# Mixture-of-experts FFN on one core: one generated order for the second stage, and a last chunk summed on VectorE

## The chip, the core and the metric

The kernel runs on one core of a Trainium2 chip. The metric is the device time of one execution in microseconds (us). The kernel before was executed three times: 1330.82 us in the median, 1330.12 to 1331.53. TensorE is PE in the profile, VectorE is DVE, ScalarE is ACT, GpSimd is POOL and SyncE is SP. SP and POOL issue the DMAs.

## What is computed

```
q = relu(cond @ W3 + b3)                      # 128 batches x 512
h = relu(((64 * x + sum_tokens(x)) * q) @ W2 + b2)   # 8192 tokens x 512
shared = (silu(h @ sw_gate) * (h @ sw_up)) @ sw_down # 704 wide
routed: each token goes to its 6 best of 64 experts, at most 64 tokens an expert,
        y[e] = (silu(buf[e] @ w_gate[e]) * (buf[e] @ w_up[e])) @ w_down[e]   # 352 wide, f32
out = x + shared + sum over a token's experts of score * y
```

## The kernel before

The 8192 tokens are 16 chunks of 512. **The first stage** computes h and the routing of all chunks, and the shared expert of the eight odd chunks, whose result is added to x on VectorE and stored by SP (`load_xr`, L357, `take_down`, L837, `store_out`, L362). The x of the even chunks is copied to the output by DMA (`keep_x`), and their h goes to memory and back (`store_hT`, `load_hT`, L340).

**The second stage**, from about 672 us on, is what the change touches. It computes the shared expert of the eight even chunks (v = 8 to 15 in the code) together with the 64 experts, which go in 32 pairs p. For a chunk, TensorE does 11 tiles `gu_tile` (12 matmuls of 512 columns each, L1163 to L1165) and 4 tiles `down_tile` (17 such matmuls, L1163 to L1165 and L1270, L1271). Between two such tiles stands either a visit `experts(p)`, that is `expert_down(p - 1)` (12 matmuls, L1410) and `expert_gate_up(p)` (32 matmuls, L1387), or a `turn(p)`, that is three transposes of the product of pair p (L1396) and four of the gathered rows of pair p + 1 (L1369). There are 33 visits (the first has no down part, the last no gate part) and 32 turns.

The order is written out by hand, once for each engine, in `unit(u)` for seven chunks and `last_unit()` for the last one. A unit holds four visits, after gu tiles 2, 6 and 10 and after down tile 2. The last unit ends with visit 31 after gu tile 9, a turn after gu tile 10, down tile 0, the last visit `experts(32)`, and down tiles 1 to 3.

The shared tiles use three PSUM banks in turn, so down tile 3 waits until VectorE has taken down tile 0 (`down_taken`). VectorE takes a down tile with `take_down` (L845, a copy to the `outst` buffers in the second stage), and scales an expert pair's result by its scores with `scale_y` (L1088). Three row buffers `hg` and three result buffers `ysc` go round.

**The sums into the output** are all made by DMAs that GpSimd issues, each behind the landing of the one before (semaphore `added`), since they can meet in a row. For a pair: `gather` of the rows for pair p + 3 (L498), then `scatter`, two indirect accumulating DMAs of 64 rows each (L509, the first with `idx_pair`, the second with `idx_hi`). For a chunk: `add_out`, two accumulating DMAs of 256 rows each (L519), both issued behind the same sum, after the scatter of the third pair of the unit; in the last unit after the last scatter. `sums_after(p)` counts the sums. At the end both SP and GpSimd wait for the last sum.

SP loads the weights: `load_down(p)` (one set of buffers) behind the down matmuls of pair p - 1, `load_gate(p + 2)` and `load_up(p + 2)` (two sets) behind the gate and up matmuls of pair p, and the next chunk's h (L340) behind every fourth pair.

Of the kernel before, what the change touches and what calls it, by code (L numbers as in the profile page):

```python
# [12 lines left out]
P = 128  # L13
# [7 lines left out]
def adaln_moe_ffn_kernel(nc, x, cond, W3, b3, W2, b2, gate_w, w_gate, w_up, w_down,  # L21
# [28 lines left out]
    PPC = NP // ND  # L50
    assert P == 2 * CAP and N == CAP and TAIL == P // 2 and B == P and E == 64 and NP == PPC * ND and PPC == 4

# [10 lines left out]
    with ctx:  # L63
# [189 lines left out]
        out_stored = [sem(f"out_stored{n}") for n in range(2)]  # L253
        gathered = [sem(f"gathered{n}") for n in range(3)]
# [49 lines left out]
        def sums_after(p):  # L304


            return 2 * (p + 1) + 2 * min((p + 1) // PPC, ND - 1)

# [10 lines left out]
        def _(sp):  # L319
# [144 lines left out]
            for p in range(NP):  # L464
                if p > 0:
                    load_down(p)
                if p + 2 < NP:
                    load_gate(p + 2)
                    load_up(p + 2)
                if p % PPC == 1 and p // PPC + 1 < ND:  # L470
                    load_hT(p // PPC + 1)
            for q in range(2):
                sp.wait_ge(out_stored[q], 32 * ND)
            sp.wait_ge(s.x_kept, 16 * ND)
            sp.wait_ge(s.pads_stored, 32)
            sp.wait_ge(s.added, 16 * (2 * NP + 2 * ND))

        @block.gpsimd
        def _(pool):
# [22 lines left out]
            def after_sums(count):  # L502
                wait(pool, s.added, 16 * count)

            def scatter(p):
                for e, idx in ((0, idx_pair[0:CAP, p:p + 1]), (1, idx_hi[:, p:p + 1])):
                    pool.wait_ge(s.y_ready, p + 1)
                    after_sums(sums_after(p) - 2 + e)
# [25 lines left out]
            for p in range(NP):  # L534
                pool.wait_ge(s.y_ready, p + 1)
                if p + 3 < NP:
                    gather(p + 3)
                scatter(p)
                if (p % PPC == PPC - 2 and p < NP - 2) or p == NP - 1:
                    for half in range(2):  # L540
                        add_out(ND + p // PPC, half)
            pool.wait_ge(s.added, 16 * (2 * NP + 2 * ND))

        @block.scalar
        def _(act):
# [164 lines left out]
            def unit(u):  # L710
                v, p = ND + u, PPC * u
                silu(v, 0)
                split_a(v, 0)
                if u == 0:
                    take_rowsT(0)
                silu(v, 1)
                silu_expert(p)
                split_a(v, 1)
                silu(v, 2)
                take_rowsT(p + 1)  # L720
                split_a(v, 2)
                silu(v, 3)
                silu_expert(p + 1)
                split_a(v, 3)
                silu(v, 4)
                take_rowsT(p + 2)
                split_a(v, 4)
                silu(v, 5)
                split_a(v, 5)
                silu_expert(p + 2)  # L730
                take_rowsT(p + 3)
                split_h(u + 1)
                silu_expert(p + 3)
                take_rowsT(p + 4)

            def last_unit():
                v, p = 2 * ND - 1, NP - PPC
                silu(v, 0)
                split_a(v, 0)
                silu_expert(p)  # L740
                silu(v, 1)
                take_rowsT(p + 1)
                split_a(v, 1)
                silu(v, 2)
                silu_expert(p + 1)
                split_a(v, 2)
                take_rowsT(p + 2)
                silu(v, 3)
                silu_expert(p + 2)
                split_a(v, 3)  # L750
                take_rowsT(p + 3)
                silu(v, 4)
                split_a(v, 4)
                silu_expert(p + 3)
                silu(v, 5)
                split_a(v, 5)

            split_h(0)
            for u in range(ND - 1):
                unit(u)  # L760
            last_unit()

        @block.vector
        def _(dve):
# [68 lines left out]
            def take_down(v, j):  # L833
                dve.wait_ge(s.down_filled, J * v + j + 1)
                if v < ND:
                    dve.wait_ge(xr_loaded[j % 2], 16 * (2 * v + j // 2 + 1))
                    nc.vector.tensor_tensor(outst[:, j % 2, :], bank[(GT + j) % 3][:, :], outst[:, j % 2, :],  # L837
                                            ALU.add).then_inc(s.down_taken, 1)
                else:
                    u = v - ND  # L840
                    if u > 0:
                        dve.wait_ge(s.added, 16 * (sums_after(PPC * (u - 1) + PPC - 2) + 2))
# [236 lines left out]
            def scale_y(p):  # L1079
# [3 lines left out]
                if p >= 3:  # L1083
                    dve.wait_ge(s.added, 16 * sums_after(p - 3))
# [7 lines left out]
            def unit(u):  # L1092
                v, p = ND + u, PPC * u
                product(v, 0)
                split_a(v, 0)
                scale_y(p - 1)
                product_expert(p)
                product(v, 1)
                split_a(v, 1)
                take_eactT(p)  # L1100
                product(v, 2)
                split_a(v, 2)
                scale_y(p)
                product_expert(p + 1)
                product(v, 3)
                split_a(v, 3)
                take_eactT(p + 1)
                product(v, 4)
                product(v, 5)
                split_a(v, 4)  # L1110
                split_a(v, 5)
                scale_y(p + 1)
                product_expert(p + 2)
                take_down(v, 0)
                take_eactT(p + 2)
                for k in range(KC):
                    split_h(NCH + u + 1, k)
                take_down(v, 1)
                take_down(v, 2)
                scale_y(p + 2)  # L1120
                product_expert(p + 3)
                take_down(v, 3)
                take_eactT(p + 3)

            def last_unit():
                v, p = 2 * ND - 1, NP - PPC
                product(v, 0)
                split_a(v, 0)
                scale_y(p - 1)
                product_expert(p)  # L1130
                take_eactT(p)
                product(v, 1)
                split_a(v, 1)
                scale_y(p)
                product_expert(p + 1)
                product(v, 2)
                take_eactT(p + 1)
                split_a(v, 2)
                scale_y(p + 1)
                product_expert(p + 2)  # L1140
                product(v, 3)
                take_eactT(p + 2)
                split_a(v, 3)
                product(v, 4)
                split_a(v, 4)
                scale_y(p + 2)
                product_expert(p + 3)
                product(v, 5)
                split_a(v, 5)
                take_eactT(p + 3)  # L1150
                take_down(v, 0)
                scale_y(p + 3)
                for j in range(1, J):
                    take_down(v, j)

            for u in range(ND - 1):
                unit(u)
            last_unit()

        @block.tensor  # L1160
        def _(pe):
# [260 lines left out]
            def unit(u):  # L1422
                v, p = ND + u, PPC * u
                gu_tile(v, 0)
                gu_tile(v, 1)
                if u == 0:
                    rowsT(0)
                gu_tile(v, 2)
                experts(p)
                gu_tile(v, 3)  # L1430
                gu_tile(v, 4)
                turn(p)
                gu_tile(v, 5)
                gu_tile(v, 6)
                experts(p + 1)
                gu_tile(v, 7)
                gu_tile(v, 8)
                turn(p + 1)
                gu_tile(v, 9)
                gu_tile(v, 10)  # L1440
                experts(p + 2)
                down_tile(v, 0)
                turn(p + 2)
                down_tile(v, 1)
                down_tile(v, 2)
# [68 lines left out]
```

## Time and profile before

| what | value |
|---|---|
| median of 3 executions | 1330.82 us |
| the profiled execution | 1330.82 us, span 1329.0 us |
| PE busy | 1291.3 us, 97% |
| DVE, ACT, POOL busy | 662.7, 370.6, 172.6 us |
| granted TensorE clock, mean | 0.988 |
| chain that ended last | 95% PE |
| HBM read and written | 196.09 MB, 61.10 MB |

The span runs from the first to the last instruction of the profiled execution; 1.8 us of its time lie outside. Busy times say how long an engine worked, not whether it was waited for. The starts of the matmuls are measured, their ends are modelled (a matmul of 512 columns is listed with 0.39 us while the next one starts 0.23 us after it), so stalls of PE are read from the distance of starts.

### The profile page before, as it was taken

To read this page: it belongs to the slowest core of one execution; us is meant where nothing else is said; L and a number is where in the kernel's file an instruction comes from. 1 tells how busy PE (TensorE), PEld (TensorE's weight loads), DVE (VectorE), ACT (ScalarE), POOL (GpSimd) and SP (SyncE) were. 2 spreads that over 40 slices of the span, in tenths; PEclk is the share of its full clock that TensorE was granted. 3 is DMA by queue.
4 is the path that set the end of the run, shared out by engine and by line. 5 is a ranking of instruction groups with operands and counts; after the bars stand their busy time and mean duration, and the time that the engine had idled before them with its cause. 6 is when DMAs were issued, how large, how long until landed. Compare 5 with 4: busy or idle time off the path is not lost.

```text
span 1329.0 us, 16619 instructions
## 1 busy us (share of the span) xinstructions
PE 1291.3 (97%) x6424; PEld 962.7 (72%) x6424; DVE 662.7 (50%) x1430; ACT 370.6 (28%) x611; POOL 172.6 (13%) x131
## 2 busy tenths in 40 slices
PE   4899999999999999999999999999999999999995
PEld 3688888888888888888876666666666666666663
DVE  6685775858768585774743223232322323323221
ACT  2634343343433434443311111121211211111110
POOL 2400000000000000000001222222222122221221
PEclk7999999999999999999999999999999999999997
DMA  6424305052250423404746797997988788797973
GB/s 202 169 101 157 105 36 193 33 175 88 77 186 4 170 88 123 139 17 153 275 169 227 250 305 256 268 318 197 317 289 248 263 260 314 234 312 251 298 210 44
DMA packets 96398, 249.89 MB, mean 188 GB/s; under 512 B 17536, under 2 KB 17664, under 8 KB 94144
## 3 DMA queue, kind: packets, MB, share of 16 engines
q1 hardware_dynamic: 84288, 222.61, 46.9%
q0 software_dynamic: 12032, 26.22, 10.1%
q8 instruction: 52, 0.85, 0.3%
q14 instruction: 26, 0.21, 0.0%
HBM read 196.09 MB, written 61.10 MB: 194 GB/s over the span
## 4 chain that ended last, share of the span: by engine, by line
PE 95%; DMA 1%; DVE 1%; issue 1%; ACT 1%; SPq 0%; POOL 0%; POOLq 0%; ACTq 0%
PE bank L1163 22%; PE bank L1165 22%; PE bank L1164 22%; PE bank L1387 11%; PE bank L1410 7%; PE bank L1197 2%; PE bank L1173 2%; PE bank L1369 1%; PE bank L1271 1%; PE bank L1270 1%; PE bank L1221 1%; PE bank L1210 1%; PE bank L1211 1%; PE bank L1396 1%; DMA stage<-in_L_cond_W_dram 1%
## 5 line engine op out<-in xcount | busy, mean ns | idle before, releaser
L1163 PE MATMUL bank<-hh,gu 128*128 128x512 f32 x704 | 280.9, 399 | 0.0
L1165 PE MATMUL bank<-hh,gu 128*128 128x512 f32 x704 | 274.7, 390 | 0.0
L1164 PE MATMUL bank<-hl,gu 128*128 128x512 f32 x704 | 274.3, 390 | 0.0
L1163 PEld LDWEIGHTS bank<-hh,gu 128*128 128x128 f32 x704 | 132.6, 188 | 35.1 <-issue 9.8
L1165 PEld LDWEIGHTS bank<-hh,gu 128*128 128x128 f32 x704 | 132.2, 188 | 28.5
L823 DVE TENSOR_TENSOR prod<-bank,prod 128x512 f32<-128x512 f32 x96 | 66.2, 690 | 172.6 <-PE bank L1165 144.9
L1164 PEld LDWEIGHTS bank<-hl,gu 128*128 128x128 f32 x704 | 132.4, 188 | 25.4
L547 ACT ACTIVATE ah<-prod 128x512 fp32r<-128x512 f32 x96 | 60.7, 632 | 275.1 <-DVE prod L823 275.1
L498 POOL DMA_INDIRECT hg<-table,idx_pair x32 | 32.9, 1029 | 787.4 <-DVE idx_hi L1033 606.4
L1163 PE MATMUL bank<-sdh,ah 128*128 128x512 f32 x320 | 128.7, 402 | 0.0
L1165 PE MATMUL bank<-sdh,al 128*128 128x512 f32 x320 | 124.9, 390 | 0.0
L1164 PE MATMUL bank<-sdl,ah 128*128 128x512 f32 x320 | 124.8, 390 | 0.0
L1163 PE MATMUL bank<-xmh,w2h 128*128 128x512 f32 x256 | 105.5, 412 | 1.8 <-DVE xml L766 1.3
L1165 PE MATMUL bank<-xmh,w2l 128*128 128x512 f32 x256 | 101.3, 396 | 0.0
L1164 PE MATMUL bank<-xml,w2h 128*128 128x512 f32 x256 | 100.7, 394 | 0.0
L590 ACT ACTIVATE prod<-bank 128x512 f32<-128x512 f32 x96 | 57.3, 596 | 130.4 <-PE bank L1165 130.1
L766 DVE TENSOR_TENSOR hl<-h,hh 128x512 fp32r<-128x512 f32 x96 | 66.8, 717 | 46.4 <-ACT hh L547 46.2
L1410 PE MATMUL bank<-wd,eactT 128*64 128x512 f32 (+1 forms) x384 | 89.6, 601 | 0.0
L1088 DVE TENSOR_SCALAR ysc<-bank,hg 64x512 f32<-64x512 f32 x64 | 48.0, 750 | 69.4 <-PE bank L1410 62.0
L563 ACT ACTIVATE h<-bank,b2c 128x512 f32<-128x512 f32 x64 | 43.9, 686 | 137.2 <-PE bank L1165 137.2
L1387 PE MATMUL bank<-wg,hgt 128*64 128x352 f32 x512 | 81.3, 459 | 0.0
L1387 PE MATMUL bank<-wu,hgt 128*64 128x352 f32 x512 | 81.2, 459 | 0.0
(123 smaller groups left out, 1708.4 us busy)
## 6 DMA issues: line engine op xcount, KB each, us to landing
wg<-in_L_ffn_w_gate_dram SPq DMA_DIRECT2D x64, 704.0 KB, 9.3
wu<-in_L_ffn_w_up_dram SPq DMA_DIRECT2D x64, 704.0 KB, 10.9
wd<-in_L_ffn_w_down_dram SPq DMA_DIRECT2D x64, 512.0 KB, 5.2
x<-in_x_dram SPq DMA_DIRECT2D x16, 1024.0 KB, 8.7
table<-hrow SPq DMA_DIRECT2D x16, 1024.0 KB, 4.4
wd<-in_L_ffn_w_down_dram SPq DMA_DIRECT2D x64, 192.0 KB, 6.1
hT<-h SPq DMA_DIRECT2D x8, 1024.0 KB, 3.9
outst<-in_x_dram SPq DMA_DIRECT2D x32, 256.0 KB, 5.1
```

The costliest lines, as they stand in the source:

```text
L498: nc.gpsimd.indirect_dma_start(out=hg[p % 3][:, :], out_offset=None, in_=table, in_offset=bass.IndirectOffsetOnAxis(ap=idx_pair[:, p:p + 1 ...
L547: return nc.scalar.activation(o, i, ACT.Copy)
L563: nc.scalar.activation(h32[:, oc, :], bank[5 + oc % 2][:, :], ACT.Relu, bias=b2c[:, oc:oc + 1]).then_inc(s.cond_taken, 1)
L590: nc.scalar.activation(prod[0:m, i % 2, :], bank[t % 3][0:m, :], ACT.Silu).then_inc(s.silu_ready, 1)
L766: return nc.vector.tensor_tensor(o, full, high.bitcast(F32), ALU.subtract)
L823: nc.vector.tensor_tensor(prod[0:m, i % 2, :], bank[t % 3][up0:up0 + m, :], prod[0:m, i % 2, :], ALU.mult).then_inc(s.prod_ready, 1)
L1088: op = nc.vector.tensor_scalar(ysc[p % 3][rows, :], bank[6][rows, :], hg[p % 3][rows, at:at + 1], None, ALU.mult)
L1163: nc.tensor.matmul(o, st_h, mv_h, start=first_mm, stop=False)
L1164: nc.tensor.matmul(o, st_h, mv_l, start=False, stop=False)
L1165: return nc.tensor.matmul(o, st_l, mv_h, start=False, stop=last_mm)
L1387: op = nc.tensor.matmul(o[half, 0:I], hgt[:, k, half], w[p % 2][e][:, k * I:(k + 1) * I], start=(k == 0), stop=(k == KC - 1))
L1410: op = nc.tensor.matmul(bank[6][half, :], eactT[0:m, it, half], wd[e][0:m, it, :], start=(it == 0), stop=(it == IT - 1))
```

## The change

One generator, `second_stage()`, gives the order of the second stage to all engines. It goes through the tiles of the eight chunks and counts work done: 12/17 for a gu tile, 1 for a down tile. Visit p comes after the first tile at which the count has reached 2.0 + 2.7 p, turn p after the first at which it has reached 2.0 + 2.7 (p + 0.5) (a visit goes first where both are due). VectorE and ScalarE follow the same order. SP loads the next chunk's h after gu tile 1 of a chunk. GpSimd issues the first half of a chunk's `add_out` after down tile 1 and the second half after down tile 3, each behind the sum before it. The last chunk has no `add_out`: when the 78 sums have landed, SP loads its four slices of 128 rows from the output into the `outst` buffers, VectorE adds each down tile to its slice in `take_down`, and SP stores the slice. ScalarE's list is generated in the same way and is left out here, as are the removed hand-written lists.

```diff
--- before.py
+++ after.py
@@ -48,6 +48,7 @@
+    GU_SHARE, FIRST_EXPERTS, EXPERTS_APART = 12 / 17, 2.0, 2.7
@@ -301,10 +303,34 @@
-        def sums_after(p):
-            return 2 * (p + 1) + 2 * min((p + 1) // PPC, ND - 1)
+        def second_stage():
+            done, p, turned = 0.0, 0, 0
+            for v in range(ND, 2 * ND):
+                for n in range(GT + J):
+                    yield ("gate_up", v, n) if n < GT else ("down", v, n - GT)
+                    done += GU_SHARE if n < GT else 1.0
+                    if v == ND and n == 1:
+                        yield "rows", 0, 0
+                    if p <= NP and done >= FIRST_EXPERTS + p * EXPERTS_APART:
+                        yield "experts", p, 0
+                        p += 1
+                    elif turned < p and turned < NP and done >= FIRST_EXPERTS + (turned + 0.5) * EXPERTS_APART:
+                        yield "turn", turned, 0
+                        turned += 1
+        sums, after_scatter, after_add = 0, {}, {}
+        for kind, n, j in second_stage():
+            if kind == "experts" and n > 0:
+                sums += 2
+                after_scatter[n - 1] = sums
+            if kind == "down" and n < 2 * ND - 1 and j % 2 == 1:
+                sums += 1
+                after_add[n, j // 2] = sums
+        SUMS = sums
@@ -461,19 +487,28 @@  (sync)
-            for p in range(NP):
-                if p > 0:
-                    load_down(p)
-                if p + 2 < NP:
-                    load_gate(p + 2)
-                    load_up(p + 2)
-                if p % PPC == 1 and p // PPC + 1 < ND:
-                    load_hT(p // PPC + 1)
+            for kind, n, j in second_stage():
+                if kind == "gate_up" and j == 1 and n + 1 < 2 * ND:
+                    load_hT(n + 1 - ND)
+                if kind == "experts" and 0 < n < NP:
+                    load_down(n)
+                if kind == "experts" and n + 2 < NP:
+                    load_gate(n + 2)
+                    load_up(n + 2)
+
+            sp.wait_ge(s.added, 16 * SUMS)
+            at = chunk_of(2 * ND - 1) * CH
+            for j in range(J):
+                rows = of[at + j * P:at + (j + 1) * P, :]
+                sp.dma_start(down_place(2 * ND - 1, j), rows).then_inc(last_loaded[j], 16)
+            for j in range(J):
+                rows = of[at + j * P:at + (j + 1) * P, :]
+                sp.wait_ge(s.down_taken, J * (2 * ND - 1) + j + 1)
+                sp.dma_start(rows, down_place(2 * ND - 1, j)).then_inc(out_stored[j % 2], 16)
@@ -499,22 +534,18 @@  (gpsimd)
             def add_out(v, half):
                 pool.wait_ge(s.down_taken, J * v + 2 * half + 2)
-                after_sums(sums_after(PPC * (v - ND) + PPC - 2 if v < 2 * ND - 1 else NP - 1))
+                pool.wait_ge(s.added, 16 * (after_add[v, half] - 1))
@@ -531,15 +562,15 @@
-            for p in range(NP):
-                pool.wait_ge(s.y_ready, p + 1)
-                if p + 3 < NP:
-                    gather(p + 3)
-                scatter(p)
-                if (p % PPC == PPC - 2 and p < NP - 2) or p == NP - 1:
-                    for half in range(2):
-                        add_out(ND + p // PPC, half)
-            pool.wait_ge(s.added, 16 * (2 * NP + 2 * ND))
+            for kind, n, j in second_stage():
+                if kind == "experts" and n > 0:
+                    pool.wait_ge(s.y_ready, n)
+                    if n + 2 < NP:
+                        gather(n + 2)
+                    scatter(n - 1)
+                if kind == "down" and (n, j // 2) in after_add and j % 2 == 1:
+                    add_out(n, j // 2)
+            pool.wait_ge(s.added, 16 * SUMS)
@@ -832,14 +826,16 @@  (vector)
-                if v < ND:
-                    dve.wait_ge(xr_loaded[j % 2], 16 * (2 * v + j // 2 + 1))
-                    nc.vector.tensor_tensor(outst[:, j % 2, :], bank[(GT + j) % 3][:, :], outst[:, j % 2, :],
+                if v < ND or v == 2 * ND - 1:
+                    if v < ND:
+                        dve.wait_ge(xr_loaded[j % 2], 16 * (2 * v + j // 2 + 1))
+                    else:
+                        dve.wait_ge(last_loaded[j], 16)
+                    nc.vector.tensor_tensor(down_place(v, j), bank[(GT + j) % 3][:, :], down_place(v, j),
                                             ALU.add).then_inc(s.down_taken, 1)
@@ -1089,73 +1085,21 @@
-            def unit(u):
...
-            for u in range(ND - 1):
-                unit(u)
-            last_unit()
+            for kind, n, j in second_stage():
+                if kind == "gate_up" and (j % 2 == 1 or j == GT - 1):
+                    product(n, j // 2)
+                    split_a(n, j // 2)
+                    if j == GT - 1 and n + 1 < 2 * ND:
+                        for k in range(KC):
+                            split_h(NCH + n + 1 - ND, k)
+                if kind == "experts":
+                    scale_y(n - 1)
+                    if n < NP:
+                        product_expert(n)
+                if kind == "turn":
+                    take_eactT(n)
+                if kind == "down":
+                    take_down(n, j)
@@ -1483,9 +1373,17 @@  (tensor)
-            for u in range(ND - 1):
-                unit(u)
-            last_unit()
+            for kind, n, j in second_stage():
+                if kind == "gate_up":
+                    gu_tile(n, j)
+                if kind == "down":
+                    down_tile(n, j)
+                if kind == "rows":
+                    rowsT(0)
+                if kind == "experts":
+                    experts(n)
+                if kind == "turn":
+                    turn(n)
```

## Rows read from the trace of the kernel before

**Rows 1.** Busy time by stretch: from:to, length, busy of each engine, clock, DMA share, GB/s

```profile
1100.00:1200.00 100.00, 100.00 (x511) 65.75 (x509) 29.41 (x50) 17.46 (x32) 23.68 (x18) 1.00 0.87 285
1200.00:1300.00 100.00, 100.00 (x521) 62.86 (x519) 30.88 (x53) 15.51 (x28) 23.64 (x18) 1.00 0.76 241
1300.00:1329.00 29.00, 12.91 (x57) 9.65 (x53) 3.57 (x5) 0.00 (x0) 5.35 (x4) 0.76 0.31 46
```

**Rows 2.** Timeline of PE, a visit, gu tiles and a turn: start us, duration us, instruction

```profile
1019.96 2.80 PE L1410 MATMUL bank<-wd,eactT 128*64 128x512 f32 x12
...
1027.42 0.50 PE L1163 MATMUL bank<-hh,gu 128*128 128x512 f32 x1
...
1028.00 0.39 PE L1165 MATMUL bank<-hh,gu 128*128 128x512 f32 x1
...
1032.77 0.40 PE L1165 MATMUL bank<-hh,gu 128*128 128x512 f32 x1
1033.00 0.49 PE L1396 MATMUL bank<-ident,eact 128*128 128x128 f32 x3
...
1033.73 0.48 PE L1163 MATMUL bank<-hh,gu 128*128 128x512 f32 x1
```

**Rows 3.** Timeline of the end, all engines

```profile
1298.33 2.80 PE L1410 MATMUL bank<-wd,eactT 128*64 128x512 f32 x12
...
1301.17 1.51 DVE L1088 TENSOR_SCALAR ysc<-bank,hg 64x512 f32<-64x512 f32 x2 [2.05 <-PE bank L1410]
...
1303.44 1.40 POOL L509 DMA_INDIRECT out_dram<-ysc,idx_pair  x1 [6.50 <-DVE ysc L1088]
...
1309.13 1.40 POOL L509 DMA_INDIRECT out_dram<-ysc,idx_hi  x1 [4.29 <-DMA out_dram<-ysc,idx_pair]
...
1312.52 0.39 PE L1271 MATMUL bank<-sdl,ah 128*128 128x512 f32 x1
1312.95 0.69 DVE L845 COPY outst<-bank 128x512 f32<-128x512 f32 x1 [3.16 <-PE bank L1271]
1313.33 2.56 POOL L519 DMA_DIRECT2D out_dram<-outst  x2 [2.80 <-DMA out_dram<-ysc,idx_hi]
```

**Rows 4.** The chain that ended last, in order of time: start us, us, what

```profile
1303.44 4.94 DMA out_dram<-ysc,idx_pair
...
1309.13 3.67 DMA out_dram<-ysc,idx_hi
```

**Rows 5.** DMA to landing of the output's DMAs from 1290 us on

```profile
DMA to landing us min/median/max: 3.7/5.4/8.3
```

**Rows 6.** The program's last line, L63: ns min/median/max, first and last start us

```profile
L63 POOLq COMPARE_BRANCH  x1: 41/41/41, 1322.4 to 1322.4; - x1
...
L63 POOLq DRAIN  x1: 6193/6193/6193, 1322.6 to 1322.6; - x1
L63 SPq DRAIN  x1: 13/13/13, 1322.7 to 1322.7; - x1
L63 SPq EVENT_SEMAPHORE  x1: 17/17/17, 1329.0 to 1329.0; - x1
```

**Rows 7.** Loads of x slices, 256 KB each (line L357)

```profile
DMA to landing us min/median/max: 2.6/5.1/8.8
```

**Rows 8.** Stores of output slices, 256 KB each (line L362)

```profile
DMA to landing us min/median/max: 2.0/4.2/8.6
```

**Rows 9.** VectorE on a down tile (tile outst): ns min/median/max

```profile
L837 DVE TENSOR_TENSOR outst<-bank,outst x32: 672/691/692, 119.1 to 680.1; 128x512 f32<-128x512 f32 x32
```

**Rows 10.** Timeline of POOL over one pair and one chunk's add_out

```profile
985.15 1.01 POOL L498 DMA_INDIRECT hg<-table,idx_pair  x1 [7.88 <-DVE ysc L1088]
986.46 1.42 POOL L509 DMA_INDIRECT out_dram<-ysc,idx_pair  x1 [0.30 <-issue]
996.04 1.40 POOL L509 DMA_INDIRECT out_dram<-ysc,idx_hi  x1 [8.16 <-DMA out_dram<-ysc,idx_pair]
1000.20 2.56 POOL L519 DMA_DIRECT2D out_dram<-outst  x2 [2.76 <-DMA out_dram<-ysc,idx_hi]
...
1011.59 1.50 POOL L509 DMA_INDIRECT out_dram<-ysc,idx_pair  x1 [4.79 <-DMA out_dram<-outst]
```

**Rows 11.** DMA issues, 1000 to 1200 us: count, KB each, median us to landing

```profile
wd<-in_L_ffn_w_down_dram SPq DMA_DIRECT2D x20, 192.0 KB, 6.3
out_dram<-outst POOLq DMA_DIRECT2D x6, 512.0 KB, 8.0
...
hg<-table,idx_pair POOLq DMA_INDIRECT x10, 8.0
```

More of the change, by code:

```diff
@@ L253, in adaln_moe_ffn_kernel @@
         out_stored = [sem(f"out_stored{n}") for n in range(2)]
+        last_loaded = [sem(f"last_loaded{n}") for n in range(J)]
         gathered = [sem(f"gathered{n}") for n in range(3)]
@@ L302, in logits_bank @@
             return bank[3] if n % 2 == 0 else bank[6]
-        def sums_after(p):
-            return 2 * (p + 1) + 2 * min((p + 1) // PPC, ND - 1)
+        def second_stage():
[12 more added lines that the diff above has]
+                        turned += 1
+            assert p == NP + 1 and turned == NP
+        sums, after_scatter, after_add = 0, {}, {}
[7 more added lines that the diff above has]
+        SUMS = sums
         def down_place(v, j):
@@ L462, in _ @@
             store_out(v, 3)
-            for p in range(NP):
-                if p > 0:
-                    load_down(p)
-                if p + 2 < NP:
-                    load_gate(p + 2)
-                    load_up(p + 2)
-                if p % PPC == 1 and p // PPC + 1 < ND:
-                    load_hT(p // PPC + 1)
+            for kind, n, j in second_stage():
[15 more added lines that the diff above has]
+                sp.dma_start(rows, down_place(2 * ND - 1, j)).then_inc(out_stored[j % 2], 16)
             for q in range(2):
-                sp.wait_ge(out_stored[q], 32 * ND)
+                sp.wait_ge(out_stored[q], 32 * (ND + 1))
             sp.wait_ge(s.x_kept, 16 * ND)
             sp.wait_ge(s.pads_stored, 32)
-            sp.wait_ge(s.added, 16 * (2 * NP + 2 * ND))
         @block.gpsimd
@@ L500, in gather @@
                     in_offset=bass.IndirectOffsetOnAxis(ap=idx_pair[:, p:p + 1], axis=0)).then_inc(gathered[p % 3], 16)
-            def after_sums(count):
-                wait(pool, s.added, 16 * count)
             def scatter(p):
+                pool.wait_ge(s.y_ready, p + 1)
                 for e, idx in ((0, idx_pair[0:CAP, p:p + 1]), (1, idx_hi[:, p:p + 1])):
-                    pool.wait_ge(s.y_ready, p + 1)
-                    after_sums(sums_after(p) - 2 + e)
+                    wait(pool, s.added, 16 * (after_scatter[p] - 2 + e))
                     nc.gpsimd.indirect_dma_start(
@@ L533, in _ @@
             pool.wait_ge(s.x_kept, 16 * ND)
-            for p in range(NP):
-                pool.wait_ge(s.y_ready, p + 1)
-                if p + 3 < NP:
-                    gather(p + 3)
-                scatter(p)
-                if (p % PPC == PPC - 2 and p < NP - 2) or p == NP - 1:
-                    for half in range(2):
-                        add_out(ND + p // PPC, half)
-            pool.wait_ge(s.added, 16 * (2 * NP + 2 * ND))
+            for kind, n, j in second_stage():
[7 more added lines that the diff above has]
+            pool.wait_ge(s.added, 16 * SUMS)
         @block.scalar
@@ L708, in silu_expert @@
                 nc.scalar.activation(esilu[:, :], bank[3][:, 0:I], ACT.Silu).then_inc(s.esilu_ready, 1)
-            def unit(u):
[L711 to L714, printed above, removed]
-                    take_rowsT(0)
[L716 to L758, printed above, removed]
-            for u in range(ND - 1):
-                unit(u)
-            last_unit()
+            split_h(0)
+            for kind, n, j in second_stage():
+                if kind == "gate_up":
+                    if j % 2 == 0:
+                        silu(n, j // 2)
+                    if j % 2 == 1 or j == GT - 1:
+                        split_a(n, j // 2)
+                    if j == GT - 1 and n + 1 < 2 * ND:
+                        split_h(n + 1 - ND)
+                if kind == "rows":
+                    take_rowsT(0)
+                if kind == "experts" and n < NP:
+                    silu_expert(n)
+                if kind == "turn":
+                    take_rowsT(n + 1)
         @block.vector
@@ L834, in take_down @@
                 dve.wait_ge(s.down_filled, J * v + j + 1)
-                if v < ND:
-                    dve.wait_ge(xr_loaded[j % 2], 16 * (2 * v + j // 2 + 1))
-                    nc.vector.tensor_tensor(outst[:, j % 2, :], bank[(GT + j) % 3][:, :], outst[:, j % 2, :],
+                if v < ND or v == 2 * ND - 1:
[4 more added lines that the diff above has]
+                    nc.vector.tensor_tensor(down_place(v, j), bank[(GT + j) % 3][:, :], down_place(v, j),
                                             ALU.add).then_inc(s.down_taken, 1)
                 else:
-                    u = v - ND
-                    if u > 0:
-                        dve.wait_ge(s.added, 16 * (sums_after(PPC * (u - 1) + PPC - 2) + 2))
+                    if v > ND:
+                        dve.wait_ge(s.added, 16 * after_add[v - 1, j // 2])
                     elif j < 2:
@@ L1083, in scale_y @@
                 if p >= 3:
-                    dve.wait_ge(s.added, 16 * sums_after(p - 3))
+                    dve.wait_ge(s.added, 16 * after_scatter[p - 3])
                 for e in range(2):
@@ L1090, in scale_y @@
                 op.then_inc(s.y_ready, 1)
[L1092 to L1154, printed above, removed]
@@ L1156, in _ @@
-            for u in range(ND - 1):
-                unit(u)
-            last_unit()
+            for kind, n, j in second_stage():
+                if kind == "gate_up" and (j % 2 == 1 or j == GT - 1):
+                    product(n, j // 2)
+                    split_a(n, j // 2)
+                    if j == GT - 1 and n + 1 < 2 * ND:
+                        for k in range(KC):
[8 more added lines that the diff above has]
+                    take_down(n, j)
@@ L1420, in turn @@
                 rowsT(p + 1)
[L1422 to L1445, printed above, removed]
-                experts(p + 3)
-                down_tile(v, 3)
-                turn(p + 3)
-            def last_unit():
-                v, p = 2 * ND - 1, NP - PPC
-                gu_tile(v, 0)
-                gu_tile(v, 1)
-                experts(p)
-                gu_tile(v, 2)
-                turn(p)
-                gu_tile(v, 3)
-                gu_tile(v, 4)
-                experts(p + 1)
-                gu_tile(v, 5)
-                turn(p + 1)
-                gu_tile(v, 6)
-                experts(p + 2)
-                gu_tile(v, 7)
-                turn(p + 2)
-                gu_tile(v, 8)
-                gu_tile(v, 9)
-                experts(p + 3)
-                gu_tile(v, 10)
-                turn(p + 3)
-                down_tile(v, 0)
-                experts(NP)
-                for j in range(1, J):
-                    down_tile(v, j)
             v = ND - 1
@@ L1485, in _ @@
             pe.wait_ge(s.slots_ready, 1)
-            for u in range(ND - 1):
-                unit(u)
-            last_unit()
+            for kind, n, j in second_stage():
+                if kind == "gate_up":
+                    gu_tile(n, j)
+                if kind == "down":
+                    down_tile(n, j)
+                if kind == "rows":
+                    rowsT(0)
+                if kind == "experts":
+                    experts(n)
+                if kind == "turn":
+                    turn(n)
 _INS = ['x', 'cond_1024', 'L0_cond_W3', 'L0_cond_b3', 'L0_cond_W2', 'L0_cond_b2', 'L0_ffn_gate_w',
```

## The prediction

> **What bounds the kernel now.** I read the busy time by stretch first. In the second stage PE is busy 100.00 of every 100 us at a granted clock of 1.00, the full one of its two levels, 2.4 GHz [rows 1]. Since ends of matmuls are modelled, I then looked in the timeline at their starts: the 21 steps from 1028.00 to 1032.77 us take 4.77 us, so 0.227 us for each shared matmul, and the next item follows without a gap [rows 2]. Prices of the stage: a gu tile 12 x 0.227 = 2.7 us, a down tile 17 x 0.227 = 3.9 us, a visit 1027.42 - 1019.96 = 7.5 us, a turn 33.73 - 33.00 = 0.7 us [rows 2]. No DMA, bank or engine is waited for, although the DMA engines are busy 0.87 of the time. So no new order can make this stage shorter; it can only keep it or put stalls into it. What can be gained stands behind the matmuls: of the last 29.0 us PE works 12.91 [rows 1]. The timeline shows this end as a chain: the last visit's down part is over at 1298.33 + 2.80 = 1301.1, scale_y runs from 1301.17, the last pair's first scatter is issued at 1303.44 and the second at 1309.13, and only then, at 1313.33, the two halves of the last chunk's sum, although PE's last matmul started at 1312.52 and VectorE took its tile from 1312.95 [rows 3]. The second half is issued some 0.8 us after the first and takes the longest landing of this stretch, 8.3 us [rows 5], which puts it at 1322.4: there GpSimd's last wait ends, and a drain of GpSimd of 6.19 us follows before the closing barrier at 1329.0 [rows 6].
>
> **The change, part by part.**
>
> *The order on PE.* The same items in another order: 88 gu tiles, 32 down tiles, 33 visits, 32 turns, all still between shared tiles. Visits come 2.7 units of work apart, where a unit of work is 3.9 us (a down tile), so with 8.2 us for visit and turn about every 10.4 + 8.2 = 18.6 us, against 11.76 / 4 = 2.94 units or 19.6 us in the units before. I take 0 us for PE: its work is the cover and ends at 1312.5 + 0.4 = 1312.9 as before. The waits that could break this are costed next.
>
> *Weights.* The cover of their loads shrinks. Placing the tiles by the generator's rule, the shortest distance between two visits is 16.0 us (a visit, two down tiles and a turn, as between visits 20 and 21). The down weights are the tight ones: issued when the down matmuls are through, 2.8 us into a visit, landing 6.3 us after issue in the median [rows 11]; with about 2 us to issue the four they are there some 11 us into the distance. The cover is about 5 us; cost 0. Demand rises by 19.6 / 18.6, so the DMA share of 0.87 to about 0.91. The h of the next chunk is asked for after gu tile 1 and needed after gu tile 10: over 30 us.
>
> *VectorE and ScalarE.* Each follows PE's order, so neither waits for something that PE does later. The new place that matters is behind gu tile 10, where four splits of h now stand ahead of the take of down tile 0. The splits cost about 4 x 0.7 = 2.8 us and down tile 3 needs that take only three down tiles or 11.6 us after gu tile 10; cost 0.
>
> *GpSimd's sums.* This is a chain of landings, off PE's path but near its pace. A pair takes 1.3 us for the gather, 996.04 - 986.46 = 9.6 us for the first scatter and 4.2 us for the second; both halves of an add_out, issued together, 1011.59 - 1000.20 = 11.4 us [rows 10]. A pair is 15.1 us, or 13.8 where the queue lags, since the gather is then issued under a landing. Before: 4 x 15.1 + 11.4 = 72 us of a unit's 4 x 19.6 = 78. After: the halves stand singly, up to 8.0 us each [rows 11], and there are 11.76 / 2.7 = 4.36 pairs in a chunk: 4.36 x 13.8 + 16 = 76.2 us, at the lagging price, of 78 + 0.36 x 8.2 = 81 us. This fits, with 5 us to spare. When the queue lags, gathers are late first: a gather takes 8.0 us to land [rows 11] and is needed a distance and a half later, which leaves 12 us or more. Cost 0, with the other end of this estimate as the third rival.
>
> *The end.* After the generator's count the last chunk begins at 7 x 11.765 = 82.35, and the last visit is due at 2 + 2.7 x 32 = 88.4, so after gu tile 8 (88.71). Behind it stand 2 gu and 4 down tiles, 92 matmuls, where before stood 3 down tiles, 51. The visit thus ends 41 x 0.227 = 9.3 us earlier, at 1291.8. The same chain as before (scale_y, scatter of 4.94 us, scatter of 3.67 us [rows 4], with the issues between) then has the last sum landed at 1309.13 + 3.67 - 9.3 = 1303.5. There SP issues four loads of 256 KB. Such a load lands after 2.6 us at best and 5.1 in the median [rows 7]; nothing else moves, so I take 3: the first slice is there at 1306.5 and, with the add of 0.69 us (as long as the copy that it replaces [rows 3, 9]), down tile 0 is taken at 1307.2. Down tile 3 wants its bank at 1312.9 - 3.9 = 1309.0: a margin of 1.8 us (-0.3 with the median landing). The other slices are in time for 1312.95. After it: 0.69 for the add, 0.1 to issue, and a store that lands in 2.0 us at best, 4.2 in the median among other traffic [rows 8]; I take 2.5, near the best. That is 1316.2.
>
> *The drain.* GpSimd no longer ends last. It waits for the 78th sum at 1303.5, and its 6.19 us then run to about 1309.9, under PE's matmuls. SP's own drain takes 0.013 us [rows 6]. Of the 6.6 us from the last landing to the end 0.4 remain. The changed span is 1316.2 + 0.4 = 1316.6, that is 12.4 us less than 1329.0: about 6.2 by the landing and 6.2 by the drain. The profiled execution took 1330.82 us, as the median did, so I forecast 1330.8 - 12.4 = 1318.4 us.
>
> The Trainium skill speaks against half of that: "VectorE: DVE Perf Modes", section "The DRAIN you can't avoid", calls the runtime's drains constant at about 12 ns on all engines. SP's row agrees; GpSimd's row of 6193 ns does not, and the row decides.
>
> **The rivals.**
>
> *The fixed end stays.* The 6.2 us may belong not to GpSimd's queue but to the end of the last DMA, whoever issued it. For it: it begins 0.2 us after the last landing. Against it: it is GpSimd's row alone, while SP is through in 0.013 us [rows 6]. Then only the landing moves: 1318.4 + 6.2 = 1324.6. With drains of 12 ns, as the skill has them, the 6.2 us would be such a rest, which gives this same time.
>
> *The last chunk's rows come late.* Scatters at their busy prices of 9.6 and 4.2 in place of 5.7 and 3.7 [rows 3, 4, 10] end 4.4 us later, at 1307.9; the first slice is then taken at 1311.6, down tile 3 waits 2.6 us, and with a slower store it is 1318.4 + 3 to 4 = 1322. Against it: no weights are loaded any more by then, as at the end before.
>
> *GpSimd's chain is over the pace (slower than before).* Place: the scatters between chunks 10 and 15. It decides from pairs of (81 - 16) / 4.36 = 14.9 us. With pairs of 15.8 us (2 us more, by the fuller DMA engines) it is 4.36 x 15.8 + 16 = 84.9, 3.6 over; seven chunks gather 25 us, 12 of them covered by the gathers' slack, so 13 us of stalls on PE, and the lag delays the last sum by a few more: 1318.4 + 13 + 2 = 1333 us. For it: the sum of 76.2 is near the 81, and every term in it is a landing beside heavy traffic. Against it: the 8.0 us of a half are measured with both halves in flight, so a single one should be shorter, and what lags is caught up in the last chunk, which has no add_out.
>
> *Weights late at the short distances.* The cover of 5 us is used up at perhaps a handful of the 16 us distances, 1 to 3 us each: 1324 to 1331.
>
> **How the numbers follow.** A measurement of this kernel can tell 0.2% or 2.7 us from no change. Forecast 0.68, its own range 1317 to 1320 (store landing 2.0 to 4.2, first load 2.6 to 5.1). Fixed end 0.09 and late rows 0.09, both faster; late weights 0.05, of which 0.02 end within 0.2%; chain over pace 0.09, slower. Faster 0.68 + 0.09 + 0.09 + 0.03 = 0.89, same 0.02, slower 0.09. The range runs from 1316.5 (best landings and the 0.7 us by which executions differ) to 1325.5, which holds the first two rivals and leaves out 0.14.
>
> **What would show it.** In the changed profile: GpSimd's drain near 1304 and about 6 us long; the last PE matmul near 1312.5; the last L1410 group ending near 1292; loads into outst issued near 1303.5; the end within 0.5 us of the last store's landing. Wrong would be: PE steps of more than 0.23 us inside the stage, waits of PE's queue for gathers or for a result's scaling, a gap before down tile 3 of the last chunk, or a drain that moves to the end with SP's last store.

## The result and the profile after

The changed kernel takes 1317.43 us in the median (1316.32 to 1318.17, 4 runs) beside 1331.07 us of the kernel before on the same chip: a ratio of 0.9899 (95% interval 0.9886 to 0.9911), faster by 1.0% or 13.6 us. The forecast was 1318.4 us, its range 1316.5 to 1325.5. The profiled execution took 1318.17 us with a span of 1316.3 us.

Busy time by stretch of the changed kernel (from:to, length, busy of each engine, clock, DMA share, GB/s) answers to [rows 1]:

```profile
1000.00:1100.00 100.00, 100.00 (x513) 66.06 (x511) 29.01 (x50) 16.85 (x30) 23.45 (x18) 1.00 0.91 301
1100.00:1200.00 100.00, 100.00 (x512) 64.59 (x513) 30.22 (x51) 17.00 (x30) 22.01 (x17) 1.00 0.83 274
1200.00:1300.00 100.00, 100.00 (x505) 66.34 (x502) 30.89 (x52) 17.25 (x30) 24.27 (x19) 1.00 0.66 196
1300.00:1317.00 17.00, 13.07 (x58) 10.51 (x56) 3.24 (x5) 0.00 (x0) 0.00 (x0) 0.95 0.43 132
```

PE is as full as before. The time in which it does not work has shrunk from 29.0 - 12.9 = 16.1 us behind 1300 us to 16.3 - 13.1 = 3.2 (the last row reaches 0.7 us beyond the span, which ends at 1316.3). The same end in the timeline, against [rows 3]:

```profile
1289.20 2.80 PE L1354 MATMUL bank<-wd,eactT 128*64 128x512 f32 x12
...
1292.04 1.51 DVE L1084 TENSOR_SCALAR ysc<-bank,hg 64x512 f32<-64x512 f32 x2 [3.38 <-PE bank L1354]
1294.31 1.41 POOL L541 DMA_INDIRECT out_dram<-ysc,idx_pair  x1 [10.71 <-DVE ysc L1084]
1298.19 1.41 POOL L541 DMA_INDIRECT out_dram<-ysc,idx_hi  x1 [2.47 <-DMA out_dram<-ysc,idx_pair]
...
1301.90 1.76 SPq L503 DMA_DIRECT2D outst<-out_dram  x4
...
1304.65 1.45 DVE L834 TENSOR_TENSOR outst<-bank,outst 128x512 f32<-128x512 f32 x2 [4.18 <-DMA outst<-out_dram]
1305.37 8.79 SPq L507 DMA_DIRECT2D out_dram<-outst  x4
...
1309.26 0.69 DVE L834 TENSOR_TENSOR outst<-bank,outst 128x512 f32<-128x512 f32 x1 [3.16 <-PE bank L1215]
...
1312.68 0.39 PE L1215 MATMUL bank<-sdl,ah 128*128 128x512 f32 x1
1313.11 0.69 DVE L834 TENSOR_TENSOR outst<-bank,outst 128x512 f32<-128x512 f32 x1 [3.16 <-PE bank L1215]
```

The last visit's down part now ends at 1292.0 instead of 1301.1. The last sum lands at 1301.9, where SP issues the loads, under PE's matmuls. The last matmul starts at 1312.68, 0.16 us later than before: nothing of PE's work was saved. The program's last line (L63 before, now L64; ns, then first and last start in us), against [rows 6]:

```profile
L64 POOLq DRAIN  x1: 5907/5907/5907, 1302.1 to 1302.1; - x1
...
L64 SPq COMPARE_BRANCH  x1: 38/38/38, 1315.9 to 1315.9; - x1
L64 SPq DRAIN  x1: 13/13/13, 1316.1 to 1316.1; - x1
L64 SPq EVENT_SEMAPHORE  x1: 17/17/17, 1316.2 to 1316.2; - x1
```

GpSimd's drain runs from 1302.1 to 1308.0 and costs nothing. The last store lands at 1315.9 and the span ends 0.4 us behind it. So of the 12.7 us of span the last landing gave 1322.4 - 1315.9 = 6.5, and the drain 6.2.

### The profile page after: what moved, and what is told of

Read it like the earlier page. It is cut to its first block, busy times and chain, and to the rows that moved or that the text cites. A ratio compares the mean times of both kernels' runs of the same rounds, so it can differ in the third digit from the quotient of the medians.

```text
span 1316.3 us, 16591 instructions
## 1 busy us (share of the span) xinstructions
PE 1291.7 (98%) x6424; PEld 962.8 (73%) x6424; DVE 663.3 (50%) x1430; ACT 370.2 (28%) x611; POOL 169.2 (13%) x129
## 4 chain that ended last, share of the span: by engine, by line
PE 97%; DVE 1%; ACT 1%; DMA 0%; issue 0%; SPq 0%; ACTq 0%; DVEq 0%
PE bank L1107 23%; PE bank L1109 22%; PE bank L1108 22%; PE bank L1331 12%; PE bank L1354 7%; PE bank L1141 2%; PE bank L1117 2%; PE bank L1313 1%; PE bank L1215 1%; PE bank L1214 1%; PE bank L1165 1%; PE bank L1154 1%; PE bank L1155 1%; PE bank L1340 1%; DVE xm L800 0%; DMA w3s<-in_L_cond_W_dram 0%
```

## The experiments

All times are medians, compared with the kernel before on the same chip in the same rounds (1330.73 us for the first four experiments, 1330.5 for the others). The changed kernel's 1317.43 us come from rounds of their own (beside 1331.07 us), so a difference of less than about 1 us between it and a variant says nothing. "Span" is that of the profiled execution. Diffs are against the changed kernel unless they say otherwise.

### The new order with the old end

```diff
-                if kind == "down" and n < 2 * ND - 1 and j % 2 == 1:
+                if kind == "down" and j % 2 == 1:
                     sums += 1
                     after_add[n, j // 2] = sums
...
-            for j in range(J):
-                rows = of[at + j * P:at + (j + 1) * P, :]
-                sp.dma_start(down_place(2 * ND - 1, j), rows).then_inc(last_loaded[j], 16)
...
-                if v < ND or v == 2 * ND - 1:
+                if v < ND:
```

> The changed kernel with its new order, but the last chunk summed as before by two accumulating DMAs of GpSimd (each behind the sum before it). Theory (the gain sits in the end, the order alone gains almost nothing): the second half can be issued only when down tile 3 is taken, about 1314.3 us into the span, lands after some 5.9 us (the shorter landing of such a half, measured before), and GpSimd's drain of 6.2 us and 0.4 us follow: span 1326.8, so 10.5 us over the changed kernel's 1316.3 and 2.2 us under the 1329.0 before. Rival (the new order itself makes the stage shorter): the span stays within 3 us of 1316.3. Sign: the last PE matmul starts at 1312.5 to 1312.7 in both.

Measured: 1327.82 us, ratio 0.9977 (0.9967 to 0.9988), span 1326.7. GpSimd in the timeline, and its drain:

```profile
1306.21 1.29 POOL L542 DMA_DIRECT2D out_dram<-outst  x1 [6.72 <-DVE outst L830]
1313.91 1.21 POOL L542 DMA_DIRECT2D out_dram<-outst  x1 [6.42 <-DVE outst L830]
```

```profile
L64 POOLq COMPARE_BRANCH  x1: 41/41/41, 1320.3 to 1320.3; - x1
L64 POOLq DRAIN  x1: 6071/6071/6071, 1320.4 to 1320.4; - x1
```

The order alone is worth 0.2%: the first half of the last chunk's sum goes out under PE's work, so only one half (6.3 us from issue to landing) stands behind the last matmul where two stood before. The rest of the gain is in the new end.

### GpSimd's drain put behind the last store

```diff
             pool.wait_ge(s.added, 16 * SUMS)
+            for q in range(2):
+                pool.wait_ge(out_stored[q], 32 * (ND + 1))
```

> The changed kernel, with GpSimd made to wait at its end until SP's last stores have landed. Theory (the 6 us belong to GpSimd's own drain and are hidden only because GpSimd is through early): the drain starts behind the last landing at 1315.9 and the span is 1315.9 + 0.15 + 6.2 + 0.2 = 1322.4, 6.1 us over 1316.3. Rival (the time had belonged to the landing of an accumulating DMA, and is gone with it): drain short, span within 1 us of 1316.3.

Measured: 1323.58 us, ratio 0.9942 (0.9926 to 0.9959), span 1322.1. The program's last line:

```profile
L64 SPq DRAIN  x1: 13/13/13, 1315.9 to 1315.9; - x1
L64 POOLq DRAIN  x1: 5907/5907/5907, 1316.0 to 1316.0; - x1
L64 SPq EVENT_SEMAPHORE  x1: 17/17/17, 1322.0 to 1322.0; - x1
```

The last store is SP's and the drain is as long as ever, although GpSimd's own last DMA had landed at 1301.5, 14.5 us before it. The 6 us belong to GpSimd's own end, and half of the gain is that GpSimd ends early: 1323.6 - 1317.4 = 6.2 us by the medians, 1322.1 - 1316.3 = 5.8 by the spans.

### The kernel before without GpSimd's last wait

Diff against the kernel before:

```diff
                         add_out(ND + p // PPC, half)
-            pool.wait_ge(s.added, 16 * (2 * NP + 2 * ND))
```

> The kernel before with one line out: GpSimd's wait for the last sum at its end. SP still waits for it. Theory A (the drain is a fixed piece of GpSimd's work, whatever is in flight): it starts at about 1316.0, when the last add is issued, ends at 1322.2, and the span ends 0.5 us behind the last landing of 1322.4, at 1322.9: 6.1 us under 1329.0. Theory B (the drain waits for the DMAs that GpSimd issued and then takes its 6.2 us): no change, 1329.0. Theory C (the drain is one wait until the DMAs are done, of whatever length): also 1322.9, but with a drain row of 6.4 us or more that ends with the landing.

Measured: 1328.39 us, ratio 0.9982 (0.9973 to 0.9992), span 1327.0. The program's last line:

```profile
L63 POOLq DRAIN  x1: 13177/13177/13177, 1313.6 to 1313.6; - x1
L63 SPq COMPARE_BRANCH  x1: 38/38/38, 1322.2 to 1322.2; - x1
```

None of the three theories holds. The drain lasts 13.2 us; it ends at 1326.7, 4.6 us behind the landing at 1322.1 (SP's branch follows it at once), where a drain that starts with everything landed takes 5.9 to 6.2. So it does not end with the landing, nor is it a fixed piece that can be laid beside transfers of its own: of its 6 us some 1.5 can. What it waits for inside these 4.6 us stays open. To hide all of it, GpSimd's last DMA has to be landed some 5 to 6 us before the end by these rows (an estimate: no run tried a distance between 0 and 12 us); in the changed kernel it is landed 14 us before. Leaving out a wait is not enough.

### Visits 2.75 apart

```diff
-    GU_SHARE, FIRST_EXPERTS, EXPERTS_APART = 12 / 17, 2.0, 2.7
+    GU_SHARE, FIRST_EXPERTS, EXPERTS_APART = 12 / 17, 2.0, 2.75
```

> The changed kernel with visits 2.75 apart in place of 2.7: the last visit moves from behind gu tile 8 to behind gu tile 10, so four down tiles (15.4 us) are left in place of 20.9. Theory (the end has a margin: in the changed kernel down tile 0 is taken at 1305.3 and down tile 3 starts at 1309.1, so 3.7 us): the visit ends 5.5 us later, so do the sums and the loads, the take of down tile 0 ends at 1310.8, down tile 3 starts 1.8 us late, and the span is 1318.1, 1.8 us over 1316.3. With the busy prices of the scatters it would be up to 4 us more. Rival (the loads of the rows are not near the path): within 0.5 us of 1316.3.

Measured: 1321.98 us, ratio 0.9931 (0.9914 to 0.9947), span 1321.6: 5.3 us over the changed kernel by the spans, 4.6 by the medians, where 1.8 was expected. The profiled execution is the slowest of the four (1323.39 us; the others took 1321.67 to 1322.05), so its trace may show a little more than the usual loss. PE in the timeline, from the last matmul of down tile 2 on, and the stretches behind it:

```profile
1309.02 0.39 PE L1215 MATMUL bank<-sdl,ah 128*128 128x512 f32 x1
1312.59 0.50 PE L1107 MATMUL bank<-sdh,ah 128*128 128x512 f32 x1 [3.19 <-DVE outst L834]
...
1314.40 0.63 PE L1107 MATMUL bank<-sdh,ah 128*128 128x512 f32 x1
1314.83 0.63 PE L1108 MATMUL bank<-sdl,ah 128*128 128x512 f32 x1
```

```profile
1313.00:1314.00 1.00, 1.00 (x6) 0.77 (x5) 0.29 (x1) 0.00 (x0) 0.00 (x0) 0.85 0.91 346
1314.00:1315.00 1.00, 1.00 (x4) 0.81 (x3) 0.57 (x1) 0.00 (x0) 0.00 (x0) 0.50 0.88 338
1315.00:1317.00 2.00, 2.00 (x7) 1.51 (x6) 0.13 (x1) 0.00 (x0) 0.00 (x0) 0.50 0.43 164
```

The direction was right and the size wrong, for two reasons. The second scatter took 5.3 us to land where the changed kernel's took 3.7, so down tile 3 started 1312.59 - 1309.02 - 0.23 = 3.3 us late and not 1.8. And after this wait of PE the granted clock fell to 0.50, that is 1.2 GHz, from 1313.7 to 1317.1 us: matmul starts stood 0.43 us apart instead of 0.23, which adds eight times 0.2 = 1.6 us. With 0.2 us by which this order brings PE later to down tile 3 anyway, that is 5.1 of the 5.3 us. A late load in this place costs its delay and then some; the margin of the changed kernel (tile 0 taken at 1305.3, wanted at 1309.06) is worth having.

### Only the last chunk squeezed

```diff
-            done, p, turned = 0.0, 0, 0
+            unit = "g g R g E g g T g g E g g T g g E d T d d E d T"
+            last = "g E g T g E g T g E g T g E g T g E g g d d d d"
...
```

(g and d are gu and down tiles, E a visit, T a turn, R the first `rowsT`, which only the first chunk has; `unit` is the hand order of the kernel before. The tuple is yielded for each letter; all else is the changed kernel.)

> The changed kernel with its new end, but the hand order of the kernel before for the first seven chunks of the stage; only the last chunk is squeezed, with visits behind gu tiles 0, 2, 4, 6 and 8 (13.7 us apart), so the last visit stands where the changed kernel has it. Theory (the closer spacing over all chunks is needed to keep GpSimd's sums from lagging into the last chunk): five pairs of 13.8 us and more come every 13.7 us on top of a late add_out, the last sum lands some 5 us later than in the changed kernel, 1.5 of it is covered by the margin, PE waits about 3.5 us before the last down tile and then runs part of it at the lower clock: span 1321 to 1322, 5 us over 1316.3. Rival (only the last visit's place counts): within 1 us of 1316.3.

Measured: 1318.74 us, ratio 0.9915 (0.9898 to 0.9931), span 1316.3. GpSimd's last sums, SP's loads, VectorE's adds, PE's last matmul of down tile 2 and first of down tile 3, and PE's waits in the whole stage:

```profile
1296.81 1.40 POOL L548 DMA_INDIRECT out_dram<-ysc,idx_pair  x1 [3.08 <-DMA out_dram<-ysc,idx_hi]
1300.70 1.40 POOL L548 DMA_INDIRECT out_dram<-ysc,idx_hi  x1 [2.50 <-DMA out_dram<-ysc,idx_pair]
1304.22 3.09 SPq L510 DMA_DIRECT2D outst<-out_dram  x4
...
1308.14 2.01 DVE L841 TENSOR_TENSOR outst<-bank,outst 128x512 f32<-128x512 f32 x3 [8.36 <-DMA outst<-out_dram]
1308.15 0.39 PE L1222 MATMUL bank<-sdl,ah 128*128 128x512 f32 x1
1308.89 0.50 PE L1114 MATMUL bank<-sdh,ah 128*128 128x512 f32 x1 [0.35 <-DVE outst L841]
```

```profile
PE bank L1114 <- DVE outst L841: 0.3, 1, 0.3
PE bank L1320 <- DMA hg<-table,idx_pair: 0.2, 1, 0.2
```

The theory fell. The sums do lag, but by 1304.2 - 1301.9 = 2.3 us and not 5, since without weight loads a pair goes in some 8.4 us. The first load then took 3.8 us where the changed kernel's took 2.7, and PE came to down tile 3 some 0.7 us earlier, at 1308.15 + 0.23 = 1308.38. Together this uses up the whole margin of 3.7 us: down tile 3 starts 0.5 us late. The spans are equal and the intervals of the two ratios overlap. What the end needs is the place of the last visit; spreading the closer distance over all chunks gives margin (3.7 us instead of none), not time.

### Visits 2.45, 2.2 and 2.0 apart

The same line as above, with these numbers.

> The changed kernel with visits 2.45 apart: 17.7 us from visit to visit in the mean, the last visit 20 us earlier. GpSimd's sums: 4.8 x 13.8 + 16 = 82 us of 85 in a chunk; DMA share 0.87 x 19.6 / 17.7 = 0.96. Theory (both still fit, and an earlier last sum gains nothing more since the end is PE plus one store): span within 0.6 us of 1316.3. Rival (GpSimd's sums or the weights are already at their pace at 2.7): 3 us or more over it, with PE waiting on gathers or on a scaled result, or on weights.

> The changed kernel with visits 2.2 apart: 16.7 us in the mean. GpSimd's sums 5.35 x 13.8 + 16 = 90 us of 89; DMA share 0.87 x 19.6 / 16.7 = 1.02. Theory of the limit: between this and 2.0 the pace is lost, here by 0 to 11 us (2% of 534 us). If GpSimd's chain is the first limit, PE waits for gathered rows or scaled results; if the DMA engines are, for weights.

> The changed kernel with visits 2.0 apart: 15.95 us in the mean. GpSimd's sums 5.88 x 13.8 + 16 = 97 us of 94; DMA share 0.87 x 19.6 / 15.95 = 1.07. Both theories say slower than the changed kernel: GpSimd's chain by 3% of 510 us less 12 us of slack, 5 us or so; the DMA engines by 7%, 25 to 35 us. The waits of PE name which. If neither is a limit (the share of 0.87 leaves out what a fuller queue can do), within 1 us of 1316.3.

| apart | median us | ratio (95%) | span us |
|---|---|---|---|
| 2.75 | 1321.98 | 0.9931 (0.9914 to 0.9947) | 1321.6 |
| 2.7 | 1317.43 | 0.9899 (0.9886 to 0.9911) | 1316.3 |
| 2.45 | 1319.14 | 0.9913 (0.9896 to 0.9929) | 1317.3 |
| 2.2 | 1330.54 | 1.0017 (0.9995 to 1.0039) | 1326.3 |
| 2.0 | 1345.34 | 1.0113 (1.0084 to 1.0142) | 1345.8 |

The waits of PE in the second stage (us in total, times, longest), for 2.45, 2.2 and 2.0:

```profile
PE bank L1354 <- DVE eactT L1072: 1.3, 1, 1.3
```

```profile
PE bank L1313 <- DMA hg<-table,idx_pair: 5.9, 1, 5.9
PE bank L1354 <- DVE eactT L1072: 2.7, 2, 1.4
```

```profile
PE bank L1313 <- DMA hg<-table,idx_pair: 21.5, 3, 10.1
PE bank L1354 <- DVE eactT L1072: 4.0, 3, 1.4
```

PE waits for gathered rows, never for weights, although at 2.0 the DMA engines are 0.95 busy. The gather behind the longest wait at 2.0, then three stretches of that run: while this gather was under way, and behind each of the two long waits (from:to, length, busy of each engine, clock, DMA share, GB/s):

```profile
886.02 1.09 POOL L533 DMA_INDIRECT hg<-table,idx_pair  x1 [0.30 <-issue]
```

```profile
886.00:894.00 8.00, 4.34 (x23) 2.84 (x19) 1.14 (x3) 0.60 (x1) 1.09 (x1) 1.00 1.00 306
...
900.50:905.20 4.70, 4.70 (x13) 3.86 (x14) 0.00 (x0) 0.60 (x1) 1.83 (x3) 0.50 0.26 37
...
1195.90:1198.70 2.80, 2.80 (x9) 2.41 (x10) 0.00 (x0) 0.60 (x1) 0.43 (x1) 0.50 0.47 76
```

Two things meet in the long waits. GpSimd's chain of sums lags, so the gather goes out late: 6.7 us before PE wants the rows at 2.2 (the wait of 5.9), 4.3 and 3.7 us before at 2.0 (the waits of 10.1 and 8.4). And it then takes 12.5, 14.4 and 12.0 us to land, where a gather of the changed kernel takes 7.7 in the median: each was issued 0.3 us behind half an `add_out`, with a DMA share of 1.00 to 1.05. With 7.7 us the three waits would have been 1.0, 3.4 and 4.0 us (an estimate). So the lag of the chain alone is the smaller part, and which of the full DMA engines and the `add_out` ahead makes the landing long was not tried.

The wait on eactT is another cost of a close order: where a turn stands directly behind gu tile 10, with one tile before the next visit, VectorE still has its four splits to do before it can take the transposes. The generated orders have this place once at 2.45, twice at 2.2 and three times at 2.0, which is how often PE waits, and not at all at 2.7. At 2.0 the waits listed come to 25.5 us. Behind the two long ones PE worked another 4.75 and 2.95 us at half the clock, which costs half of that, 3.9 us; together this is the 29.5 us by which the span is over the changed kernel's. The kernel at 2.2 had spread-out times, 1328.05 to 1338.56 us in ten runs. Its trace is of the fastest; the three slowest had a mean granted clock of 0.988 beside 0.991, but no trace of them was kept, and why they were slower stays open.

## Why the prediction was right

*PE's work as it was.* Forecast: last matmul start 1312.5, no stall. Measured: 1312.68, no wait of PE in the second stage. The order was taken as free, and at a distance of 2.7 it is; experiments at 2.45 to 2.0 show that it was near the place where it is not. The prediction looked for trouble behind gu tile 10, where the four splits stand, but only for the take of down tile 0; what waits there in a closer order is the take of the turn's transposes, 1.3 us each time. That 2.7 has no such place was luck as far as the prediction goes, which does not look for it.

*The end.* The visit's end was forecast at 1291.8 and came at 1292.0. The last sum was forecast at 1303.5 and came at 1301.9: the first scatter was priced at 4.94 us to land [rows 4] and took 3.6, and the second was issued 0.3 us behind its landing instead of 0.75, so the margin before down tile 3 was 3.7 us and not 1.8. Here the forecast was too careful, without effect on the time. The first load was there 2.7 us after its issue (3 taken), the add took 0.69 us as forecast. The last store landed in 2.0 us, the best of the range, where 2.5 was taken: this is most of the 0.3 us by which the span is under the forecast 1316.6.

*The drain.* Forecast to run from 1303.5 to 1309.9 unseen; it ran from 1302.1 to 1308.0. The experiment that puts it behind the last store loses some 6 us again, so this half of the gain is shown and not only argued. The rival "the fixed end stays" is out. The Trainium skill ("VectorE: DVE Perf Modes", section "The DRAIN you can't avoid") calls the runtime's own drains constant at about 12 ns on all engines. SP's takes 13 ns in every run here, but GpSimd's 5744 to 6193 ns with all landed and 13177 ns with DMAs in flight. The profile gives these rows to a line of the program itself (L63, L64), so whether they are among the drains that the page speaks of is not shown; for GpSimd's the prediction was right to go by the row.

*Late rows.* This rival did not happen at 2.7, but its mechanism is real: the run at 2.75 shows it, 4.6 us by the medians. Its price left out the clock.

*GpSimd's chain.* Named as the way to slower, with 5 us to spare in a chunk. At 2.7 it keeps its pace. Two of its terms were mis-sized. A single half of an add_out was priced at up to 8.0 us and thought to be shorter; from 1000 to 1200 us it takes 11.6 in the median of five, and over the whole stage (672 to 1300 us) 9.9, where the kernel before has 9.2. The scatters took 6.8 and 4.9 us over the whole stage after 7.8 and 4.4 before, 0.5 less in sum. So the chain needs about 4.36 x 13.3 + 2 x 9.9 = 78 us of 81 (an estimate), with 3 to spare and not 5. The gather was priced at 8.0; of the twelve that were issued while a half was under way seven took 10.4 to 13.0, which the slack of 12 us or more covered. This slow landing is most of what PE waits for at 2.2 and 2.0. That the first waits appear between 2.45 and 2.2, where the expectations of these runs have the chain at 82 of 85 and 90 of 89 us, is therefore in part luck. (In this rival's own sum 84.9 us are 3.9 over 81 and not 3.6, so its stalls would be 15 us.) The DMA issues of the changed kernel (count, KB, us to landing) against [rows 11]:

```profile
out_dram<-outst POOLq DMA_DIRECT2D x5, 512.0 KB, 11.6
...
out_dram<-ysc,idx_hi POOLq DMA_INDIRECT x10, 5.7
hg<-table,idx_pair POOLq DMA_INDIRECT x10, 7.9
out_dram<-ysc,idx_pair POOLq DMA_INDIRECT x10, 7.1
```

*Weights late.* They landed as before (the 192 KB pieces in 5.8 us after 6.3), and PE waited for none in any run.

The total: 13.6 us by the medians against 12.4 forecast, the span 12.7. The 1.0 us between the forecast and the median is within what executions of this kernel differ by (1316.32 to 1318.17).

## What to carry to other kernels

When the matmul engine is full, read the span behind its last matmul row by row, the closing drains of each engine's queue among them: here 12.7 of 16 idle us could go without touching the matmuls. An engine whose queue ends with a long drain should get its last work done early, and the last transfer should be a plain store from another queue, small and alone. An order that only moves work is free until something that must land in time comes late, here gathered rows behind a chain of sums, so price that chain with the landings of a busy stretch, and leave a margin where a late transfer would make the matmul engine wait, since the wait may cost the clock as well.

## What the runs showed of the hardware that had not been expected

GpSimd's drain at the end takes 5.7 to 6.2 us with all its DMAs landed, even when they had landed 14.5 us before, and 13.2 us when it starts with two 512 KB accumulating DMAs in flight, ending 4.6 us behind their landing. After a wait of PE of 3.2 us, its clock stayed at full level for about 1.1 us of new matmuls and was then at half for 3.4 us (starts 0.43 us apart); after a wait of 3.0 us, at visits 2.0 apart, it stayed at full level throughout. The same 64-row scatter landed in 3.7 us in one kernel and 5.3 us in another, with no other data moving beside it in either. In the second stage of the changed kernel a gather issued while a 512 KB accumulating DMA was under way took 7.2 to 13.0 us to land, the others at most 9.0.
